# Sums of a softmax's second halves: a third accumulating transfer in place of four products

## The reference

```python
Q, K, V = (proj(Wq), proj(Wk), proj(Wv))
att = jnp.einsum('bhqd,bhkd->bhqk', Q, K) * (1.0 / math.sqrt(Dh)) + b[0]
att = jax.nn.softmax(att * m + (1.0 - m) * NEG_INF, axis=-1)
y = jnp.einsum('bhqk,bhkd->bhqd', att, V)
...
q = jnp.clip(jnp.round(y / scale), -128, 127)        # scale: row maximum of |y| / 127
out = x + (q @ weight.T * scale * w_scale + bias).astype(jnp.float16)
```

## Time and profile before

| | |
|---|---|
| median of three runs | 2285.32 us (2284.84 to 2288.55) |
| the profiled execution: its time, its span | 2288.77 us, 2287.0 us |
| granted clock of TensorE, mean | 0.996 |
| TensorE busy | 2264.2 us, 99% |
| GpSimd busy | 1686.9 us, 74% |
| DVE busy | 1610.9 us, 70% |
| ACT busy | 1298.3 us, 57% |
| accumulating transfers | 159 of 1024 KB, landing after 8.3 us (median) |

### The profile page before, as it was taken

One profiled execution on the slowest core, in us unless ns is written; L12 is line 12 of the kernel. 1 busy time (PEld: TensorE's weight loads), 2 busy tenths in 40 slices (PEclk: granted clock), 3 DMA queues, 4 the chain that ended last, 5 costly groups with the idle time before them and its releaser, 6 DMA issues.

```text
span 2287.0 us, 34843 instructions
## 1 busy us (share of the span) xinstructions
PE 2264.2 (99%) x12140; PEld 1376.8 (60%) x12172; DVE 1610.9 (70%) x2779; ACT 1298.3 (57%) x2471; POOL 1686.9 (74%) x704
## 2 busy tenths in 40 slices
PE   9999999999999999999999999999999999999998
PEld 7888888887555555555555555555555555555553
DVE  3311111117788888888888888888888888888883
ACT  3322222223666666666666666666666666666664
POOL 2322333222689999899998998989998899899896
PEclk9999999999999999999999999999999999999999
DMA  6765455475788888888888888888888888888864
GB/s 238 254 230 194 177 190 212 183 229 141 157 183 181 194 192 192 191 191 187 188 182 188 191 193 190 188 185 194 191 192 189 187 193 186 179 193 196 189 149 102
DMA packets 146405, 432.24 MB, mean 189 GB/s; under 512 B 13192, under 2 KB 49032, under 8 KB 125904
## 3 DMA queue, kind: packets, MB, share of 16 engines
q1 hardware_dynamic: 114000, 237.31, 36.4%
q0 software_dynamic: 22896, 166.73, 36.3%
q10 hardware_dynamic: 9360, 26.22, 3.4%
HBM read 161.51 MB, written 100.93 MB: 115 GB/s over the span
## 4 chain that ended last, share of the span: by engine, by line
PE 96%; DMA 2%; issue 1%; POOL 1%; ACT 0%; DVE 0%; ACTq 0%; POOLq 0%
PE score L793 22%; PE ring L143 20%; PE pv L819 20%; PE ring L340 11%; PE score L340 9%; PE ring L865 5%; PE pv L340 3%; PE ring L832 2%; DMA probs<-probs 1%; PE ring L830 1%; POOL acc L1145 1%; PE ring L855 1%; PE ring L165 0%; ACT probs L927 0%; PE ring L842 0%
## 5 line engine op out<-in xcount | busy, mean ns | idle before, releaser
L150 DVE TENSOR_REDUCE half_max<-ring 128x1 f32<-128x512 f32 x2048 | 1256.7, 678 | 67.6 <-PE ring L143 59.9
L927 ACT ACTIVATE probs<-score 128x512 f32<-128x512 f32 x2039 | 1033.3, 615 | 471.7 <-PE score L793 466.2
L1145 POOL TENSOR_TENSOR acc<-acc,probs 128x2048 f32<-128x2048 f32 x189 | 898.9, 4756 | 62.5 <-DMA probs<-probs 61.8
L793 PE MATMUL score<-q_stack,k_stack 100*128 100x512 f32 x2039 | 847.6, 417 | 4.7 <-ACT probs L927 4.7
L143 PE MATMUL ring<-k_stack,q_stack 98*128 98x512 f32 x2048 | 816.6, 399 | 2.4 <-issue 2.2
L793 PEld LDWEIGHTS score<-q_stack,k_stack 100*128 100x128 f32 x2039 | 384.4, 189 | 331.8 <-issue 185.5
L819 PE MATMUL pv<-probs,v_in 128*32 128x512 f32 x4096 | 495.0, 601 | 0.0
L143 PEld LDWEIGHTS ring<-k_stack,q_stack 98*128 98x128 f32 x2048 | 389.4, 190 | 70.3 <-DVE qT L1052 8.7
L1145 POOL TENSOR_TENSOR acc<-probs 128x2048 f32<-128x2048 f32 x63 | 288.0, 4571 | 53.9 <-DMA probs<-probs 47.8
L558 POOL TENSOR_TENSOR q_stack<-x_raw,k_stack 128x1024 fp32r<-128x1024 f32 x28 | 67.9, 2471 | 293.9 <-ACT k_stack L422 293.9
L819 PEld LDWEIGHTS pv<-probs,v_in 128*32 128x32 f32 x4096 | 107.1, 109 | 233.1 <-ACT probs L927 145.2
(11 more groups left out here) (117 smaller groups left out, 1986.9 us busy)
## 6 DMA issues: line engine op xcount, KB each, us to landing
probs<-probs POOLq DMA_DIRECT2D x159, 1024.0 KB, 8.3
q_stack<-qk_part SPq DMA_DIRECT2D x192, 256.0 KB, 5.7
k_stack<-qk_part SPq DMA_DIRECT2D x96, 512.0 KB
qk_part<-part_hi SPq DMA_DIRECT2D x64, 512.0 KB, 2.7
qk_part<-part_lo SPq DMA_DIRECT2D x64, 512.0 KB, 3.6
v_steps<-v_out SPq DMA_DIRECT2D x64, 256.0 KB, 2.3
v_in<-v_steps SPq DMA_DIRECT2D x32, 512.0 KB, 5.6
v_out<-x ACTq DMA_DIRECT2D x31, 512.0 KB, 3.5
```

The lines of the kernel that those rows point to most:

```text
L150: nc.vector.tensor_reduce(half_max[:, pair // CHUNK, pair % CHUNK, half:half + 1], bank[:, :], AX_X, ALU.max, negate=True).then_inc(neg_ma ...
L793: pe.matmul(score[score_bank(s, t)][:, :], k_stack[par][0:ROWS, h, kt * P:(kt + 1) * P], q_stack[par][0:ROWS, half, h, :], start=True, sto ...
L927: nc.scalar.activation(probs[:, kt, h, :], score[score_bank(s, t)][:, :], ACT.Exp).then_inc(exp_done, 1)
L1145: nc.gpsimd.tensor_tensor(acc[:, half, :, :], first, probs[:, tile, :, :], ALU.add).then_inc(acc_done, 1)
```

## The change

In second halves, tile 2 is now added onto tile 3 by a transfer, so they have three: 0 onto 1, 2 onto 3, 4 onto 5. The adds of a second half become tiles 6, 3, 5 and 7, and the four products for tile 7 go. First halves keep their transfers and adds. The pairs get a number for each of the four possible transfers, with `PAIRED` saying which half has which. In GpSimd's order the transfers 2 onto 3 and 4 onto 5 of the second half stand right behind the first half's last add, ahead of the second half's first add (tile 6); the second add (tile 3) moves to the head of the next step.

```diff
--- before.py
+++ after.py
@@ -48,14 +48,12 @@
 CHUNK = PAIRS // 2
 LOADS_K, LOADS_Q = 16 * 5, 16 * 3
 RING = 8
-PAIRS_OF_TILES = ((0, 1), (4, 5), (6, 7))
+PAIRS_OF_TILES = ((0, 1), (2, 3), (4, 5), (6, 7))
+PAIRED = ((0, 2, 3), (0, 1, 2))
 FIRST = 1
-ADDED = ((2, 3, 5, 7), (2, 3, 5, 6))
-APART = 7
+ADDED = ((2, 3, 5, 7), (6, 3, 5, 7))
 ADDS = len(ADDED[0])
 FREED = [{FIRST: 1, **{tile: k + 1 for k, tile in enumerate(added)}} for added in ADDED]
-READ_BY = {a: i for i, (a, b) in enumerate(PAIRS_OF_TILES)}
-SUMMED_BY = {b: i for i, (a, b) in enumerate(PAIRS_OF_TILES)}
 LAST = STEPS - 1
 
 OWN = 20
@@ -656,7 +654,7 @@
 
         def pairs_before(s, half, i):
 
-            return s + half if PAIRS_OF_TILES[i][1] == APART else QH * s + half
+            return s * sum(i in paired for paired in PAIRED) + half * (i in PAIRED[0])
 
         def ring_of(use):
 
@@ -825,11 +823,8 @@
                 if isinstance(s, int) and (s, half) == (0, 0):
                     pe.wait_ge(const_set, 3)
                 pe.wait_ge(acc_done, ADDS * halves_before(s, half) + ADDS)
-                if half == 1:
-                    for h in range(GH):
-                        pe.matmul(buf[h * DH:(h + 1) * DH, 0:N], ones[:, :], probs[:, APART, h, :], start=True, stop=False)
                 for h in range(GH):
-                    mm = pe.matmul(buf[h * DH:(h + 1) * DH, 0:N], ones[:, :], acc[:, half, h, :], start=half == 0, stop=True)
+                    mm = pe.matmul(buf[h * DH:(h + 1) * DH, 0:N], ones[:, :], acc[:, half, h, :], start=True, stop=True)
                 mm.then_inc(sum_done, 1)
 
             def sum_tile(tile, buf, start=False, stop=False):
@@ -919,10 +914,8 @@
                     before = halves_before(s, half) - 1
                     if kt in FREED[1 - half]:
                         wait(act, acc_done, ADDS * before + FREED[1 - half][kt])
-                    elif kt in READ_BY:
-                        wait(act, pair_done[READ_BY[kt]], 16 * pairs_before(s, half, READ_BY[kt]))
                     else:
-                        wait(act, sum_done, before + 1)
+                        wait(act, pair_done[kt // 2], 16 * pairs_before(s, half, kt // 2))
                 act.wait_ge(score_done, UNITS * s + t + 1)
                 nc.scalar.activation(probs[:, kt, h, :], score[score_bank(s, t)][:, :], ACT.Exp).then_inc(exp_done, 1)
 
@@ -1131,12 +1124,12 @@
             def add(s, half, k):
 
                 tile = ADDED[half][k]
-                if tile in SUMMED_BY:
-                    pool.wait_ge(pair_done[SUMMED_BY[tile]], 16 * (pairs_before(s, half, SUMMED_BY[tile]) + 1))
+                if tile % 2 == 1 and tile // 2 in PAIRED[half]:
+                    pool.wait_ge(pair_done[tile // 2], 16 * (pairs_before(s, half, tile // 2) + 1))
                 else:
                     pool.wait_ge(exp_done, UNITS * s + GH * (half * TT + tile + 1))
                 if k == 0:
-                    pool.wait_ge(pair_done[SUMMED_BY[FIRST]], 16 * (halves_before(s, half) + 1))
+                    pool.wait_ge(pair_done[0], 16 * (halves_before(s, half) + 1))
                     wait(pool, sum_done, halves_before(s, half) - 1)
                     first = probs[:, FIRST, :, :]
                 else:
@@ -1167,6 +1160,8 @@
 
             def step(s, par, prev=True, ahead=True):
                 second = not isinstance(s, int) or s >= 2
+                if prev:
+                    add(s - 1, 1, 1)
                 if second:
                     add_bias(s - 2, 0)
                     add_residual(s - 2, 0)
@@ -1177,22 +1172,22 @@
                     normalise(s - 1, 0)
                     add(s - 1, 1, 3)
                 add(s, 0, 0)
-                begin_pair(s, 0, 1)
+                begin_pair(s, 0, 2)
                 add(s, 0, 1)
                 if prev:
                     normalise(s - 1, 1)
                 if second:
                     add_bias(s - 2, 1)
-                begin_pair(s, 0, 2)
+                begin_pair(s, 0, 3)
                 add(s, 0, 2)
                 begin_pair(s, 1, 0)
                 if second:
                     add_residual(s - 2, 1)
                 add(s, 0, 3)
                 if ahead:
+                    begin_pair(s, 1, 1)
+                    begin_pair(s, 1, 2)
                     add(s, 1, 0)
-                    begin_pair(s, 1, 1)
-                    add(s, 1, 1)
 
             all_steps(pool, step)
             add_bias(LAST - 1, 0)
```

## The result

The changed kernel takes 2308.26 us (median of 4 runs, 2307.21 to 2317.21), the kernel before, measured beside it, 2286.62 (4 runs, 2284.84 to 2288.55). The ratio is 1.0103, 95% interval 1.0076 to 1.0130: 21.6 us slower. Predicted were 2309 us and slower.

The account below looks back on a forecast made before the run. TensorE bounds the kernel before (53.25 us a step), GpSimd's ring close behind at 51.5. Removal -26.7 us plus new waits +50.7 give +24, so 2309 us; range 2264 to 2330, the forecast's own 2292 to 2340.

Parts of the forecast that it names:

- The ring: GpSimd's cycle from T0 to T0, 46.0 us + L less 0.7: predicted 54.2 us, above TensorE's 52.39.
- L: Time from issue of T2' to its landing, ahead of the add of tile 3; claimed 8.9 us, bounds 7.1 and 10.9.
- T0: GpSimd's transfer of tile 0 onto 1 in the first half; numbers name source tiles, a prime marks the second half.
- T2': The added sixth transfer, tile 2 onto 3 in the second half; its wait before tile 3's add was called certain.
- the follower: Second half's tile 4 transfer, expected 0.6 us behind T2' on GpSimd's queue, delaying its completion: 8.9 us taken.
- The shared queue: Same-queue transfers run one after the other, so L stays near a single transfer's 8.9 us; shared engines would give near 12.
- The first 29.4 us: GpSimd from T0 to the first half's last add; its three landings shrink 0.7 us in sum, bounds 0 and 1.0.
- Where TensorE waits: TensorE waits 1.8 us a step for `acc_done`, ahead of the products with ones at line 832.
- What I priced at nothing: DVE's second-half row maximum waits 1 to 2 us on late GpSimd, TensorE behind it, within TensorE's spare 1.8 us.
- The two terms: Removed tile 7 products, 31 x 0.86, -26.7 us; TensorE's new waits, 28 steps with 1.81 us, +50.7.
- T4' late: Rival: key loads delay the second half's tile 4 transfer past tile 5's add; 2.9 us a step, about 2390; chance 0.08.
- The first rival: TensorE stays the bound, or nearly: L 7.1 to 7.7, all 26.7 us gained, 2259; without shrinking 2278; chance 0.32.

Follow-up runs that it names:

- e6: Kernel after with the four products of the second half's sums issued twice, 0.86 us a step more TensorE work: 2304.5 us, ratio 1.007.
- e11: Kernel after with the added transfer cut to two of its four heads, half of tile 2 left out of the sums: 2262.26 us, ratio 0.9891.
- e1: Kernel after with the second half's tile 4 transfer issued behind the add of tile 6: 2312.48 us, ratio 1.0102.
- e9: Kernel after with only 16 of 1024 residual columns loaded, the rest left out of the result: 2283.02 us, ratio 0.9988.
- e2: Kernel after with the second half's output store issued by SyncE instead of ACT: 2308.57 us, ratio 1.0088.
- e10: Kernel after with the small residual load of e9 and the second half's store issued by SyncE: 2270.97 us, ratio 0.9935.
- e7: Kernel before without the four products for tile 7 in second halves, nothing in their place: 2267.2 us, ratio 0.992.
- e8: Control: kernel before with the second half's store issued by SyncE instead of ACT: 2286.25 us, ratio 0.9994.
- e4: Kernel after with the added transfer issued ahead of the first half's last add, nothing left out: 2283.9 us, ratio 0.9987.
- e13: Kernel after with the residual load in two halves out of the added transfer's data, store on SyncE, nothing left out: 2292.38 us, ratio 1.0024.
- e5: Kernel after with the added transfer ahead of the first half's last add and the second half's store on SyncE: 2296.49 us, ratio 1.0039.
- e12: Kernel after with the added transfer cut to two of four heads and the second half's store on SyncE: 2256.07 us, ratio 0.9864.

## Why the prediction was right

**The ring and its bound: right, and right in size.** "46.0 us + L, less 0.7" was 54.2; measured is 54.20. Its parts fit too (means of 28 steps): the first half's last add begins 28.8 us after T0 (predicted 28.7), T2' goes out at 33.3 (33.25), the add of tile 3 begins 9.2 us behind it (9.0), and T0 comes 11.7 us after that (11.95). e6 shows that TensorE isn't the bound, e11 that the bound is L: with T2' landing in 5.61 us the ring would be 46.0 - 0.7 + 5.6 = 50.9, and the step falls to TensorE's own.

**The size of L: right number, wrong reason.** I took 8.9 us because of the follower; the mean was 8.92. But e1 took the follower out of T2's data and L stayed at 8.82, in one step with the follower wholly behind the landing, while e9 kept the follower, took the residual load out, and L fell to 7.83. The failed step is "T2' has its follower 0.6 us behind it, with a full megabyte": the follower came 2.9 us behind, and a load that I hadn't listed came between. I had looked at what follows on GpSimd's and SyncE's queues, and at the earlier trace rows for how long completions can be held; ACT's queue also issues. In the step of the earlier trace rows that load was issued at 1567.66, 4.1 us ahead of T4' and behind the data of T0': clear of both. The change put a transfer into its place. The prediction had said that it would be wrong if a second transfer right behind doesn't delay the first one's completion. That came true; that the residual load made L the same 8.9 is luck. The rest, from 7.1 in a quiet stretch to 7.8, isn't the follower either: in six of e9's 28 steps T2' landed in 6.99 to 7.05 us with T4' issued 1.6 to 2.8 us behind it. What it is, no run here tells.

**The shared queue.** By the Trainium skill (DMA: Bandwidth & Descriptors, Queues, rings and completion order) descriptors of one ring go in order, and T2' shouldn't be slowed by T4' behind it on the same ring. The runs agree: 8.82 us in e1 against 8.92, and 7.0 in e9 with T4' 1.8 us behind. The data of the residual load, on another queue, aren't ordered behind T2', and they did get in ahead of its closing packets.

**The first 29.4 us.** The sum was right (0.6 us off in place of 0.7), its items not all: T6 lands in 8.00 us (before 9.33), T0' in 7.34 (8.30), but T4 in 9.78 (9.18), and T0, for which I expected a longer landing, in 7.63 (7.39).

**Where TensorE waits: wrong.** I expected its 1.8 us ahead of the products with ones (line 832, now 827), for `acc_done`. No such wait is in the trace of after. TensorE waits for exponentials that ACT holds back while its store waits for GpSimd. The recorded 24.5 us are part of the 28 x 1.81 = 50.7; the records of lines 791 and 141 are also 5 and 11 us longer in sum than in e11. What I priced at nothing had two of these couplings: ACT's store, which I hadn't seen, and DVE's maximum of |y|, which I had. The first costs nothing while the landing of T2' is the later end (e2: 2308.57 against 2308.26), and 12 us once it mostly isn't (e9 to e10). What the second costs wasn't tested by itself; in e2 it grew to 15.0 us of TensorE's waits and the time stayed.

**The two terms: both somewhat too large.** The removal was to give 0.86 us in each of 31 steps, 26.7. In e7 most steps are as short as that (24 of 30 took 52.37 to 52.57 us), but five took 53.05 to 53.58 (and one 51.32), and the loop gained 22.0 (the time, 20.7). The waits were to cost 28 x 1.81 = 50.7; in the loop they cost 47.7, since the step without them is 52.51 and not 52.39. The two errors nearly cancel: +24 predicted, +25.8 in the loop, +21.6 in the time. The last difference lies outside the loop, which the profiled execution of after entered 6.2 us earlier than that of before, and that of e7 1.7 us earlier. Chance can give nearly as much: e8, which does the same as before up to there, entered 5.0 us earlier than it.

**T4' late.** The rival asked for a landing beyond 16.4 us. It was 12.6 on the mean and 14.6 at most (14.1 predicted), hidden in all but two of 28 steps, where GpSimd waited 0.45 and 0.87 us.

**The first rival** asked for L of 7.1 to 7.7. T2' was never under 8.0. Had the residual load been elsewhere at no cost, L would have been 7.8, and e9 puts the kernel there 3 to 5 us under before, not at 2259: by the second path, which no rival had. e10, with the store moved as well, comes nearer to it (2271).

**A gain that exists, and why it isn't had.** The change pays if its megabyte costs no waiting: 2271 in e10, 2262 in e11, both with work left out. With all the work in place the best were e4 (2283.9, no different from before) and e13 (2292.4). The sixth transfer takes the DMA engines from 0.87 to 0.93 and more. In e13 one landing grew where another was shortened; what holds e4 wasn't tested. I haven't shown that no order would do it.

## What to carry to other kernels

When work goes from a full engine to one with spare time, follow the second engine's own ring through every landing: 74% busy hid a ring that was only 1.7 us shorter than the bound. For the landing of a transfer, list what every queue issues during its data, small loads and other engines' queues too, since data that another queue moves can delay its completion. Before removing one wait, look for a second path that ends at the same time: here two changes were worth nothing and 25 us singly, and 37 together.

## What of the hardware was not expected

- A 512 KB load on ACT's queue, issued 0.9 to 2.2 us behind a 1 MB transfer of GpSimd's queue, delayed its completion by 1.1 us (8.92 against 7.83, means of 28 steps), by moving at the end of its data (75.7% of the engines against 10.4%). A second 1 MB transfer on the same queue, 2.9 us behind, delayed it by 0.1 at most (8.92, against 8.82 with 5.5 us between them).
- Half the bytes landed in 5.61 us in place of 8.92: 512 KB less are worth 3.3 us, more than half of the 5.0 us of data. The residual load was there too, issued 1.0 us behind in the step that I looked at, so its lesser harm to a short transfer is open.
- Some orders of the same work scatter much more than others: e4's ten runs lie 26 us apart, e5's ten 20 and e13's twelve 13, where all runs of the kernel before, from 2281.49 to 2291.87, lie within 10. A DMA share of 0.92 to 0.95 isn't enough to explain it, since e10 to e12 (four runs each) have it too and lie 3 to 8 us apart. The cause is open.
